# The value blocks of an attention layer: turned by VectorE and carried by way of DRAM, in place of TensorE's transposes, with new orders for every engine

## The reference, cut to what matters

```python
qkv = xn @ w_qkv.T                       # 32 q heads, 8 k, 8 v, each 128 wide
scores = einsum('bskgd,btkd->bkgst', qh, kh) / sqrt(128)
probs  = softmax(where(causal, scores, min))
attn   = einsum('bkgst,btkd->bskgd', probs, vh)     # vh: t on the contracted axis
s = attn.reshape(1, 1024, 4096) @ w_dense.T
g = silu(ffn(xn))
return x + s * g
```

## Time and profile before

| what | value |
|---|---|
| median of 3 runs | 906.7 us (905.87 to 908.21) |
| the profiled execution | 906.27 us |
| its span, first to last instruction | 904.1 us |
| granted TensorE clock | 0.999 |
| PE busy, matmuls | 894.7 us, 99% |
| DVE, ACT, POOL busy | 667.3, 519.9, 465.8 us |
| bytes moved by DMA | 143.83 MB in 204,980 packets |

### The profile page before, as it was taken

One profiled execution on the slowest core, in us unless ns is written; L12 is line 12 of the kernel. 1 busy time (PEld: TensorE's weight loads), 2 busy tenths in 40 slices (PEclk: granted clock), 3 DMA queues, 4 the chain that ended last, 5 costly groups with the idle time before them and its releaser, 6 DMA issues.

```text
span 904.1 us, 16000 instructions
## 1 busy us (share of the span) xinstructions
PE 894.7 (99%) x4297; PEld 759.5 (84%) x4297; DVE 667.3 (74%) x1162; ACT 519.9 (58%) x1096; POOL 465.8 (52%) x372
## 2 busy tenths in 40 slices
PE   8999999999999999999999999999999999999998
PEld 7888888888888888888888888888888888888886
DVE  6788866777678766878678776787667785677756
ACT  4766635764465645666366645666456663686552
POOL 4455633663454654556346634546535553346666
PEclk9999999999999999999999999999999999999999
DMA  5696656767477763955567672876548665556464
GB/s 186 187 265 179 121 114 186 213 162 149 77 206 221 149 116 97 287 141 127 106 193 215 162 150 73 211 220 139 116 120 265 146 138 93 148 147 145 105 140 152
DMA packets 204980, 143.83 MB, mean 159 GB/s; under 512 B 23168, under 2 KB 172416, under 8 KB 204928
## 3 DMA queue, kind: packets, MB, share of 16 engines
q1 hardware_dynamic: 176256, 129.68, 56.3%
...
...
## 4 chain that ended last, share of the span: by engine, by line
issue 48%; POOL 33%; PE 16%; DVE 1%; DMA 1%; POOLq 1%; ACT 0%; SPq 0%; DVEq 0%
POOL pt_lo L787 24%; POOL w_lo L799 5%; POOL wd_lo L799 3%; PE ps_m L1323 3%; PE ps_m L1162 2%; PE ps_m L1164 2%; PE ps_m L1163 2%; PE ps_s L1308 2%; PE ps_o L1162 1%; PE ps_o L1163 1%; PE ps_o L1164 1%; PE ps_s L1163 1%; PE ps_s L1164 1%; PE ps_s L1162 1%; DMA prob_odd<-x 1%
## 5 line engine op out<-in xcount | busy, mean ns | idle before, releaser
L787 POOL TENSOR_TENSOR pt_lo<-pt_lo,pt_hi 128x512 fp32r<-128x512 f32 x248 | 328.0, 1346 | 283.2 <-ACT pt_hi L909 283.0
L1006 DVE CUSTOM_DVE_ANT_0 ps_s<-ps_s,mask 128x32 f32<-128x32 f32 (+31 forms) x256 | 182.3, 713 | 115.0 <-PE ps_s L1164 113.8
L909 ACT ACTIVATE pt_hi<-pt_lo 128x512 fp32r<-128x512 f32 x288 | 169.4, 625 | 55.6 <-PE ps_o L1164 36.1
L1162 PE MATMUL ps_m<-xn_hi,w_hi 128*128 128x512 f32 (+1 forms) x392 | 153.1, 391 | 1.1 <-DVE xn_lo L1087 1.0
L1164 PE MATMUL ps_m<-xn_hi,w_lo 128*128 128x512 f32 (+1 forms) x392 | 151.3, 386 | 0.0
L1163 PE MATMUL ps_m<-xn_lo,w_hi 128*128 128x512 f32 (+1 forms) x392 | 151.3, 386 | 0.0
L1163 PE MATMUL ps_s<-k_lo,q_hi 128*128 128x480 f32 (+15 forms) x384 | 126.6, 330 | 0.0
L1164 PE MATMUL ps_s<-k_hi,q_lo 128*128 128x480 f32 (+15 forms) x384 | 126.6, 330 | 0.0
L1162 PE MATMUL ps_s<-k_hi,q_hi 128*128 128x480 f32 (+15 forms) x384 | 124.7, 325 | 0.0
L853 ACT ACTIVATE prob_even<-ps_s,small 128x32 f32<-128x32 f32 (+15 forms) x128 | 82.4, 644 | 63.1 <-DVE small L1006 61.4
L853 ACT ACTIVATE prob_odd<-ps_s,small 128x160 f32<-128x160 f32 (+15 forms) x128 | 96.0, 752 | 37.9 <-DVE small L1006 34.9
...
## 6 DMA issues: line engine op xcount, KB each, us to landing
raw<-wqkv SPq DMA_DIRECT2D x48, 256.0 KB, 4.0
...
raw<-wd SPq DMA_DIRECT2D x32, 256.0 KB, 6.1
inv_rows<-inv SPq DMA_DIRECT2D x32, 256.0 KB, 4.0
at_lo<-inv SPq DMA_DIRECT2D x32, 256.0 KB, 3.7
turned<-prob_odd SPq DMA_DIRECT2D x32, 256.0 KB, 4.3
```

The costliest lines, as they stand in the source:

```text
L787: pool.tensor_tensor(pt_lo[:, slot, :], pt_lo[:, slot, :].bitcast(F32), pt_hi[:, hi_slot, :], ALU.subtract).then_inc(land_lo, 1)
L909: act.activation(pt_hi[:, hi_slot, :], pt_lo[:, LAND_AT[i] + j, :].bitcast(F32), ACT.Copy).then_inc(land_hi, 1)
L1006: dve.tensor_tensor_reduce(out=scores, in0=scores, in1=mask[:, S - width(i % BLOCKS, tile):S], scale=-1.0, scalar=BIG, op0=ALU.add, op1=AL ...
L1162: pe.matmul(out, sta_hi, mov_hi, start=start, stop=False)
```

## The change

The values no longer pass through PE a second time. DVE transposes 32x32 squares while it takes the projection out of PSUM (`dve.transpose` into `vt` in place of `tensor_copy`). SP writes `vt` to a DRAM tensor `values` in four DMAs of 32 partitions (`vw`, pieces of 32 floats), waits until they have landed, and reads the half back in one DMA so that the tokens lie on the partitions (`vr`, pieces of 128 floats, into `v_lo`). ACT rounds `v_lo` to `v_hi` in SBUF, and POOL subtracts. `vblocks` is gone from PE and from DVE, and the shared banks have two users fewer in each body. In the prologue `vw.0` comes before `rw` and `dw`, `vr.0` between `dw` and `rr`; in the loop `vw.1`, `vr.1` stand in the middle and `vw.0`, `vr.0` last on SP, so that `hi.vblocks.0` and `lo.vblocks.0` move into the following body. All written orders of all engines are replaced by others.

```diff
 def has_hi(item):
-    return item[0] in ("vblocks", "hidden") or (item[0] == "unit" and item[1] != "v")
+    return item[0] == "hidden" or (item[0] == "unit" and item[1] != "v")
...
@@ SP, prologue @@
-    sp = [("load", p) for p in PIECES + [f"wd{h}" for h in range(HEADS)]] + [("scales",), ("rw", first), ("dw", first), ("rr", first), ("dr", first)]
+    sp = [("load", p) for p in PIECES + [f"wd{h}" for h in range(HEADS)]] + [("scales",), ("vw", 0), ("rw", first), ("dw", first), ("vr", 0), ("rr", first), ("dr", first)]
...
@@ BODY, pe the end of row 2 to row 3 @@
-        dense.0.3 scores.5.0 dense.1.0 scores.5.1 dense.1.1 dense.1.2 scores.5.2 weigh.2.0
-        dense.1.3 weigh.2.1 weigh.2.2 vblocks.1 scores.5.3 weigh.3.0 unit.q3.0.0 weigh.3.1
+        scores.5.0 dense.0.3 scores.5.1 unit.q3.0.0 unit.q3.0.1 unit.q3.0.2 unit.q3.0.3 weigh.2.0
+        weigh.2.1 weigh.2.2 scores.5.2 scores.5.3 weigh.3.0 weigh.3.1 dense.1.0 weigh.3.2
...
@@ BODY, pe the end @@
-        scores.8.1 unit.v.0.0 scores.8.2 unit.v.0.1 unit.v.0.2 weigh.7.0 weigh.7.1 unit.v.0.3
-        weigh.7.2 weigh.7.3 scores.8.3 weigh.7.4 weigh.7.5 weigh.7.6 weigh.7.7 vblocks.0 dense.6.0
-        dense.6.1 dense.6.2 dense.6.3 dense.7.0 dense.7.1 dense.7.2 dense.7.3
+        dense.5.2 dense.5.3 unit.v.0.0 unit.v.0.1 weigh.7.0 weigh.7.1 unit.v.0.2 weigh.7.2
+        weigh.7.3 weigh.7.4 weigh.7.5 unit.v.0.3 weigh.7.6 weigh.7.7 dense.6.0 dense.6.1 dense.6.2
+        dense.6.3 dense.7.0 dense.7.1 dense.7.2 dense.7.3
...
@@ BODY, act the start @@
-        hi.split.wd0 hi.split.wd1 hi.split.wd2 exp.1.0 exp.1.1 exp.1.2 exp.1.3 hi.unit.q2.1
-        exp.2.0 hi.split.wd3 hi.unit.q0.1 exp.2.1 exp.2.2 hi.split.q0 exp.2.3 hi.land.0.0 exp.3.0
+        hi.split.wd0 hi.split.wd1 hi.split.wd2 exp.1.0 exp.1.1 exp.1.2 exp.1.3 hi.unit.k.1 exp.2.0
+        hi.vblocks.0 hi.split.wd3 hi.unit.q0.1 exp.2.1 exp.2.2 hi.split.q0 exp.2.3 hi.land.0.0
...
@@ BODY, sp @@
-        load.q0 load.q1 dw.1 rw.1 load.q2 load.q3 load.k load.v dr.1 rr.1 dw.2 rw.2 dw.3 rw.3 dr.2
-        load.wd0 load.wd1 load.wd2 load.wd3 dr.3 rr.2 rr.3 move.4.0 move.4.1 move.4.2 move.4.3
-        move.5.0 move.5.1 move.5.2 move.5.3 rw.4 rw.5 rr.4 rr.5 move.6.0 move.6.1 move.6.2
-        move.6.3 rw.6 rr.6 move.7.0 move.7.1 move.7.2 move.7.3 rw.7 rr.7 dw.8 rw.8 dr.8 rr.8
+        load.q0 load.q1 dw.1 rw.1 load.q2 load.q3 load.k load.v dr.1 rr.1 dw.2 rw.2 dw.3 rw.3
+        load.wd0 dr.2 vw.1 load.wd1 load.wd2 load.wd3 dr.3 rr.2 vr.1 move.4.0 move.4.1 move.4.2
+        move.4.3 rr.3 move.5.0 move.5.1 move.5.2 move.5.3 rw.4 rw.5 rr.4 move.6.0 move.6.1
+        move.6.2 move.6.3 rw.6 rr.5 rr.6 move.7.0 move.7.1 move.7.2 move.7.3 rw.7 dw.8 rr.7 rw.8
+        dr.8 rr.8 vw.0 vr.0
...
@@ LAST, act the start @@
-        hi.split.wd0 hi.split.wd1 exp.1.0 hi.split.wd2 exp.1.1 exp.1.2 exp.1.3 hi.unit.q3.1
+        hi.vblocks.0 hi.split.wd0 exp.1.0 exp.1.1 exp.1.2 exp.1.3 exp.2.0 exp.2.1 exp.2.2
...
@@ class Run @@
+    def value_no(self, half):
+        return 1 if self.kind == "prologue" else 2 * self.g + 1 + half
+
+    def value_writes(self, half):
+        return 1 if self.kind == "prologue" else 2 * self.g + (2 if half else 3)
...
@@ SP @@
+                    elif what == "vw":
+                        half, = item
+                        sp.wait_ge(shared_read, r.shared_no(("unit", "v", half)))
+                        for n in range(CHUNKS):
+                            sp.dma_start(values_d[half, :, :, :, n, :].rearrange("j b a c -> a (j b) c"),
+                                         vt[n * Q:(n + 1) * Q, :].rearrange("a (n c) -> a n c", c=Q))\
+                              .then_inc(v_written, 16)
+                    elif what == "vr":
+                        half, = item
+                        sp.wait_ge(v_written, 16 * CHUNKS * r.value_writes(half))
+                        if kind != "prologue":
+                            sp.sem_inc(v_seen)
+                            sp.wait_ge(block_weighed, WEIGHED0 + PAIRS * g + (0 if half else pair_no(7, 3) + 1))
+                        sp.dma_start(v_lo[:, half * 4:half * 4 + 4, :].bitcast(F32),
+                                     values_d[half, :, :, :, :, :].rearrange("j b a q c -> (b a) j (q c)")).then_inc(v_landed, 16)
...
@@ POOL @@
+                    elif what == "lo" and item[0][0] == "vblocks":
+                        half = item[0][1]
+                        rows = slice(half * 4, half * 4 + 4)
+                        pool.wait_ge(v_hi_done, r.value_no(half))
+                        pool.tensor_tensor(v_lo[:, rows, :], v_lo[:, rows, :].bitcast(F32), v_hi[:, rows, :],
+                                           ALU.subtract).then_inc(v_split, 1)
...
@@ ACT @@
-                        act.wait_ge(shared_done, r.shared_no(item))
-                        act.activation(v_hi[:, half * 4:half * 4 + 4, :],
-                                       bank[:, :].rearrange("p (b d) -> p b d", d=P),
-                                       ACT.Copy).then_inc(shared_hi, 1)
+                        rows = slice(half * 4, half * 4 + 4)
+                        act.wait_ge(v_landed, 16 * r.value_no(half))
+                        act.activation(v_hi[:, rows, :], v_lo[:, rows, :].bitcast(F32),
+                                       ACT.Copy).then_inc(v_hi_done, 1)
...
@@ DVE @@
-                            dve.tensor_copy(vt[:, :], bank[:, :]).then_inc(shared_read, 1)
+                            if kind != "prologue":
+                                dve.wait_ge(v_written, 16 * CHUNKS * (r.value_writes(half) - 1))
+                            dve.transpose(vt[:, :], bank[:, :]).then_inc(shared_read, 1)
...
-                    elif name == "vblocks":
-                        half = item[1]
-                        dve.wait_ge(shared_hi, r.hi_no(item))
-                        dve.tensor_tensor(v_lo[:, half * 4:half * 4 + 4, :],
-                                          bank[:, :].rearrange("p (b d) -> p b d", d=P),
-                                          v_hi[:, half * 4:half * 4 + 4, :], ALU.subtract)\
-                            .then_inc(shared_read, 1)
...
@@ PE @@
-                            pe.wait_ge(shared_read, r.shared0)
+                            pe.wait_ge(v_split, r.value_no(0))
...
-                            pe.wait_ge(shared_read, r.shared_no(("vblocks", 1)))
+                            pe.wait_ge(v_split, r.value_no(1))
...
-                    elif name == "vblocks":
-                        for n in range(4):
-                            mm = pe.transpose(bank[:, n * P:(n + 1) * P], vt[:, n * P:(n + 1) * P],
-                                              ident[:, :])
-                        mm.then_inc(shared_done, 1)
...
+    values = nc.dram_tensor("values", (2, HALF // P, TILES, Q, CHUNKS, Q), F32).ap()
```

More of the change, by code:

```diff
@@ L149, in prologue @@
     ln = lambda *blocks: [("ln", b) for b in blocks]
-    values = [("vblocks", 0)]
     tiles = range(TILES)
@@ L153, in prologue @@
     pe = ln(0, 1) + [("warm",), ("begin", "q0")] + ln(2, 3) + [("begin", "q1")] + unit("q0")[-1:] + unit("q1")[-1:] + unit("q2") \
-        + unit("q3") + ln(4, 5) + unit("k") + ln(6, 7) + unit("v") + [("scores", first, r) for r in tiles] + values
+        + unit("q3") + ln(4, 5) + unit("k") + ln(6, 7) + unit("v") + [("scores", first, r) for r in tiles]
     units = [("unit", p, 0) for p in ("q0", "q1", "q2", "q3", "k", "v")]
@@ L164, in prologue @@
         act += [("exp", first, r)]
-    act += hi(*values)
     stats, scale = ([[(name, b) for b in range(n, n + 2)] for n in range(0, BLOCKS, 2)] for name in ("stats", "scale"))
@@ new lines @@
+        exp.3.0 exp.3.1 hi.unit.q2.1 exp.3.2 exp.3.3 hi.unit.q1.1 hi.split.q1 hi.split.q2
+        hi.land.1.0 hi.land.1.1 hi.unit.q3.1 hi.split.q3 hi.weigh.0 hi.split.k hi.split.v exp.4.0
+        exp.4.1 hi.weigh.1 exp.4.2 exp.4.3 hi.land.2.0 hi.land.2.1 hi.land.2.2 exp.5.0 exp.5.1
+        hi.unit.q3.0 hi.land.3.0 hi.land.3.1 hi.land.3.2 hi.land.3.3 hi.weigh.2 exp.5.2 exp.5.3
+        amove.4.0 amove.4.1 amove.4.2 amove.4.3 hi.vblocks.1 amove.5.0 amove.5.1 amove.5.2
+        amove.5.3 hi.land.4.0 exp.6.0 exp.6.1 hi.land.4.1 hi.land.4.2 hi.land.4.3 exp.6.2 exp.6.3
@@ L229 @@
+        mul.weigh.7 lo.weigh.7 lo.dense.6 lo.dense.7
     """,
     "pool": """
[L231 to L235 removed]
@@ L274 @@
     """,
     "act": """
-        hi.split.wd0 hi.split.wd1 exp.1.0 hi.split.wd2 exp.1.1 exp.1.2 exp.1.3 hi.unit.q3.1
-        exp.2.0 hi.split.wd3 hi.unit.q0.1 exp.2.1 exp.2.2 exp.2.3 hi.land.0.0 hi.unit.q2.1 exp.3.0
-        exp.3.1 hi.unit.k.1 exp.3.2 exp.3.3 hi.land.1.0 hi.unit.q1.1 hi.weigh.0 hi.land.1.1
-        build.0.0 build.0.1 build.0.2 build.0.3 build.1.0 exp.4.0 exp.4.1 hi.vblocks.1 build.1.1
-        build.1.2 exp.4.2 build.1.3 hi.weigh.1 hi.hidden.0.0.0 exp.4.3 hi.hidden.0.0.1 hi.land.2.0
@@ new lines @@
+        hi.unit.q1.1 exp.2.3 hi.land.0.0 hi.split.wd1 hi.unit.q2.1 hi.split.wd2 hi.split.wd3
```

(10 more changed lines are left out.)

226 lines of the change are left out of this document (111 added, 115 removed).

## The result

| | before | after |
|---|---|---|
| median of the runs | 906.7 us | 935.1 us (934.7 to 937.0, 5 runs) |
| ratio | | 1.0318 [1.0306, 1.0330] |
| the profiled execution | 906.3 us | 937.0 us |
| its span | 904.1 us | 935.1 us |
| distance between two bodies (first `scores` to first `scores`) | 104.9 to 105.3 | 114.1, 108.7, 109.3, 109.0, 106.5, 111.1, 109.2 |

The account below looks back on a forecast made before the run. The prediction took PE, a row of instructions with hardly a hole, as the bound. Its terms, -7.0 - 1.8 + 2.1 + 0.5 = -6.2, gave 900.1, as median 900.5 us; forecast range 897 to 904, eight in ten 896.0 to 911.0.

Parts of the forecast that it names:

- Term 3: Mid-body `vw.1` ahead of `dr.3` on SP's queue: landing at 37.2, `weigh.3.0` stalls 0.3 per body, 2.1 us lost.
- Rival 3: Each small write of `vw.1` costs double, `dr.3` lands at 44.3, stall 55 us, about 953; chance 0.03.
- Rival 2: `vw.1`'s packets make `dr.3` late at `weigh.3.0`; 921 at the bound; chance 0.13 slower, 0.11 within 0.3%.
- Term 1: PE loses 16 sets of four transposes, 0.44 us each: 7.0 us gained.
- Rival 4: PE's freed time turns into waits elsewhere under the new orders: no change that can be told, 906.7; chance 0.05.
- Term 2: PE's existing stall at `weigh.7.6` for POOL's row 7 subtractions, near each body's end, shrinks: 1.8 us gained.
- Term 4: First half's values crossing into the next body: free in bodies, 0.5 us lost once at the last round's start.
- The other engines: DVE's transpose costs 0 to 0.1 more, POOL's subtractions 1.35 each, ACT's rounding nothing: no price on the path.

Follow-up runs that it names:

- e4: Changed kernel with `vw.1` in its place but written in 128 pieces of 2 KB instead of 2048 of 128 B, values wrongly placed; 909.5 us.
- e7: Changed kernel with eight unused products of 512 columns added on PE in its idle time before `weigh.3.0`; 928.0 us.
- e9: Kernel before with only one of the four PE transposes in each set made, nothing else changed; 904.7 us.
- e3: Kernel before's orders with the values carried by way of DRAM, `vw.1` and `vr.1` behind `rr.2`; 910.6 us.
- e14: Changed kernel with `vw.1`, `vr.1` behind row 3's read and the first half's splitting moved to before `land.1.0`; 933.8 us.
- e16: e14 with the prologue's values written in 128 pieces of 2 KB instead of 2048 of 128 B, wrongly placed; 933.8 us.
- e17: e3 with the prologue's values transposed by PE and copied by VectorE instead of going through DRAM; 909.7 us.
- e18: Changed kernel with `vw.1`, `vr.1` behind row 3's read and the prologue's values transposed by PE instead of going through DRAM; 909.7 us.
- e2: Changed kernel's new orders, but the values go through PE's transposes as before, without `vw` or `vr`; 912.4 us.

## Why the prediction was wrong

**Term 3 failed, at the price of `vw.1`.** The prediction left `dr.3`'s issue where it was and added to its landing only the time that the 2048 pieces take of the DMA engines. That time was nearly right. SP's time to issue them, and the loads behind them, was not in the sum at all. For the engines' time, DMA in a stretch of one microsecond in which nothing else moved (250.8 to 251.8, the kernel after):

```profile
DMA packets 1039, 0.13 MB, mean 129 GB/s; under 512 B 1039, under 2 KB 1039, under 8 KB 1039
...
q1 hardware_dynamic: 1039, 0.13, 74.6%
```

That is 0.746 x 16 / 1039 = 11.5 ns for a piece of 128 B (estimated: 13), so 2048 of them are 1.5 us of 16 engines; the 1533 small pieces from 286.8 to 287.8, with reads around them, took 13 ns each (124.1% x 16 / 1533). The row of 512 B pieces gave 35 ns each. Rival 3 therefore did not happen: the prediction took the read-modify-write that the Trainium skill gives for less than 512 B (DMA: Bandwidth & Descriptors, Specifications) as the cost of two large writes, and the trace has a 128 B write at a third of one of 512 B. But SP needed 3.46 us for `vw.1`'s four issues and 2.95 for the three loads behind it, where the prediction let only the packets push `dr.3` back. `dr.3` was issued 5.4 us later, and had landed at 40.1 (39.4 in the mean of six bodies) instead of the 37.2 of the sum. A smaller slip is in the same term: the 34.7 taken for the landing before was the end of its packets, while issue and median landing time make 27.3 + 8.3 = 35.6. How the lateness divides between SP's issue and the thinner reads behind the small pieces stays open (e4). The other half of the term held: PE was ready at 39.1 (predicted 39.07). With the prediction's 37.1 for the first product a landing at 40.1 makes 3.0 us of stall there, and this body's excess is 3.0; its 36.5, for no stall at the next product either, would make 3.6. Over the seven the excess is 18.9 us, for 2.1 in the sum. Rival 2 named this place, a late `dr.3` and PE's wait for it, but by the packets' time at full engines, and priced it at 921; it had 0.24 in all, with 0.13 for slower.

**The clock was left out.** 7.2 us by e7's median, 9.7 between the profiled executions. The prediction read a clock of 1.00 in the row and did not ask what a wait of 3 us does to it. Rival 2 at 921 lacks this too.

**Term 1 was right as work and wrong as time.** The row count shows the work gone. By e9 a removed microsecond of PE gives back a third, so of 7.0 some 2.4 could come out. The prediction took the 1.8 us between row 3's landing and its latest use for slack. ACT and POOL in order of time, the kernel before, body at 244.1:

```profile
280.72 0.88 ACT L853 ACTIVATE prob_odd<-ps_s,small 128x736 f32<-128x736 f32 x1 [1.33 <-DVE small L1006]
...
281.58 2.18 ACT L909 ACTIVATE pt_hi<-pt_lo 128x512 fp32r<-128x512 f32 x4
```
```profile
282.28 5.05 POOL L787 TENSOR_TENSOR pt_lo<-pt_lo,pt_hi 128x512 fp32r<-128x512 f32 x4 [1.62 <-ACT pt_hi L909]
```

ACT copies row 3 only behind an exp that waits for VectorE's maximum, whose scores come from PE. POOL's first subtraction ends at 282.28 + 1.27 = 283.55 and PE starts its product at 283.63 without a wait in the record: the two were level. Rival 4, that freed time turns into waits elsewhere, is what e9 and e3 show; it had 0.05.

**Term 2 came at its place and gained nothing.** Before, the start of `weigh.7.6` is 0.2 to 0.4 us over normal spacing in every body and the matmul behind it 0.1. After, it stands at the normal 0.23 in all seven. But POOL still makes five subtractions of row 7 back to back, and PE now meets them elsewhere: `weigh.7.5` is 0.2 late in every body and `weigh.7.0` 0.1 to 0.8, with 0.1 each for the matmul behind. Over seven bodies that is 3.2 us before and 5.3 after. PE's weight loads in the body of 255.8, 96 and 101 us into it:

```profile
352.01 0.19 PEld L1194 LDWEIGHTS ps_o<-pt_hi,v_hi 128*128 128x128 f32 x1 [0.41 <-POOL pt_lo L818]
...
356.68 0.19 PEld L1194 LDWEIGHTS ps_o<-pt_hi,v_hi 128*128 128x128 f32 x1 [0.48 <-POOL pt_lo L818]
```

**Term 4 looked at the wrong end.** ACT does wait 5.0 us for the values from DRAM at the start of the last round, and they are in 1.4 after it (predicted 0.9), but no wait of PE follows there and the last round is 0.6 us shorter. The same trip in the prologue was not examined, and there it cost: of the first body's 8.8 us over 105.3, 4.4 are the wait at `weigh.3.0` and about 1.2 the clock. The other 3 go with the first half's values in front of row 8's write by e14 and e16, though e17 and e18 without that trip give back only about half of the first body's excess.

**The other engines** were right: VectorE's transpose out of PSUM took 0.718 us (predicted 0 to 0.1 over 0.685), POOL's subtraction 1.29.

The sum again, with measured terms: 18.9 (wait) + 7.2 (clock) + 3 (first body) - 1.8 to 2.4 (transposes) = 26.7 to 27.3. The medians differ by 28.4, but the waits are read in the profiled executions, whose spans differ by 31.0; with the clock read there too (9.7) the sum is 29.2 to 29.8 of 31.0. The new orders' 0.5 us per body in e2, of which row 7's waits are a part, may be the rest; that was not separated, and such closeness is in part luck.
